# A deformable gather's row weights: one 128-partition transfer and a two-sided clamp in place of four 32-partition transfers, an upload through TensorE and two clamps

## The reference, cut to what matters

```
off = _conv(x, ow, 1) + ob
py = clip(yy + off[:, :, 0], 0.0, H - 1)      # row coordinate of every output pixel
px = clip(xx + off[:, :, 1], 0.0, W - 1)      # column coordinate
y0, x0 = floor(py), floor(px);  wy, wx = py - y0, px - x0
out = v00*(1-wy)*(1-wx) + v01*(1-wy)*wx + v10*wy*(1-wx) + v11*wy*wx
```

## Time and profile before

| | us |
|---|---|
| runs | 5919.41, 5877.91, 5885.14 |
| median | 5885.14 |
| span of the profiled execution | 5921.8 |
| first gather, from its first row DMA to its end | 1185.8 |
| second gather | 340.1 |
| third gather | 302.7 |
| middle stage between the first and the second gather | 133.0 |
| middle stage between the second and the third | 160.2 |

### The profile page before, as it was taken

One profiled execution on the slowest core, in us unless ns is written; L12 is line 12 of the kernel. 1 busy time (PEld: TensorE's weight loads), 2 busy tenths in 40 slices (PEclk: granted clock), 3 DMA queues, 4 the chain that ended last, 5 costly groups with the idle time before them and its releaser, 6 DMA issues. The chain is left out here.

```text
span 5921.8 us, 79668 instructions
## 1 busy us (share of the span) xinstructions
PE 5032.9 (85%) x30592; PEld 2727.3 (46%) x30592; DVE 3610.3 (61%) x4317; ACT 1856.8 (31%) x2899; POOL 1464.4 (25%) x1828
## 2 busy tenths in 40 slices
PE   4877877876999799997998995999999967986987
PEld 2333333324777677766776772222222233232222
DVE  6888878885666566653222223767677765653764
ACT  2222222202222122210000003667677743641750
POOL 0222222230000000002001002555555543442540
PEclk7888888867999899998999997889799887777987
DMA  1000000001000000002211216889899968857962
GB/s 30 15 15 22 22 22 22 15 15 72 15 15 8 22 1 14 15 19 100 68 61 65 75 50 153 205 196 211 181 219 216 210 171 174 185 121 137 215 172 92
DMA packets 272018, 538.25 MB, mean 91 GB/s; under 512 B 167976, under 2 KB 169576, under 8 KB 264728
## 3 DMA queue, kind: packets, MB, share of 16 engines
q1 hardware_dynamic: 271640, 533.13, 36.3%
HBM read 419.75 MB, written 113.25 MB: 90 GB/s over the span
## 5 line engine op out<-in xcount | busy, mean ns | idle before, releaser
L1436 POOL TENSOR_SCALAR g_kw<-g_kw 128x512 f32<-128x512 f32 x1536 | 947.0, 641 | 904.3 <-ACT g_kw L1422 666.3
L1422 ACT ACTIVATE g_vw<-ps,l_index 128x512 f32<-128x512 f32 x1536 | 970.0, 685 | 409.5 <-PE ps L1478 409.4
L1455 DVE SCALAR_TENSOR_TENSOR g_prod<-g_vw,ps 128x1024 f32<-128x1024 f32 x768 | 902.7, 1217 | 271.4 <-PE ps L1493 270.8
L1296 PE MATMUL ps<-o_pad,o_ow 128*128 128x512 f32 x3456 | 851.8, 408 | 8.4 <-DVE o_pad L822 7.7
L1478 PE MATMUL ps<-g_coord,l_spread 80*128 80x512 f32 x1920 | 743.2, 489 | 125.2 <-DMA g_coord<-coords 125.1
L1093 PE MATMUL ps<-l_pair,l_w 128*128 128x512 f32 x3072 | 779.8, 403 | 0.0
L1478 PEld LDWEIGHTS ps<-g_coord,l_spread 80*128 80x128 f32 x1920 | 343.2, 213 | 906.3 <-ACT g_vw L1422 679.6
L1296 PEld LDWEIGHTS ps<-o_pad,o_ow 128*128 128x128 f32 x3456 | 656.8, 191 | 197.9 <-DVE o_pad L822 7.9
L1093 PEld LDWEIGHTS ps<-l_pair,l_w 128*128 128x128 f32 x3072 | 575.7, 191 | 156.4 <-issue 29.4
L1422 ACT ACTIVATE g_kw<-ps,l_index 128x512 f32<-128x512 f32 x384 | 264.3, 688 | 1176.3 <-PE ps L1478 1162.1
L1493 PE MATMUL ps<-g_kw,g_img 32*32 32x512 f32 x12288 | 508.9, 687 | 126.2 <-DVE g_prod L1455 100.0
(11 more groups left out here) (247 smaller groups left out, 4737.7 us busy)
## 6 DMA issues: line engine op xcount, KB each, us to landing
g_rows<-whole SPq DMA_DIRECT2D x1536, 192.0 KB, 4.9
coords<-o_parts SPq DMA_DIRECT2D x32, 1024.0 KB, 4.0
g_coord<-coords SPq DMA_DIRECT2D x96, 256.0 KB
l_x<-xcur SPq DMA_DIRECT2D x16, 1024.0 KB, 6.1
coords<-o_parts SPq DMA_DIRECT2D x32, 512.0 KB, 5.6
g_img<-dense SPq DMA_DIRECT2D x96, 128.0 KB, 4.4
gathered<-g_res SPq DMA_DIRECT2D x48, 256.0 KB, 4.7
l_xn<-in_x SPq DMA_DIRECT2D x8, 1024.0 KB, 5.0
```

The lines of the kernel that those rows point to most:

```text
L1296: ins = nc.tensor.matmul(ps[:, lo:lo + HALF], ow[:, a, kk, tap, y, k * P:(k + 1) * P], padded_rows(pad[:, m, c, kk], j, tap), start=(n == ...
L1422: nc.scalar.activation(to, bank(a % RING), ACT.Relu, bias=index[:, 0:1]).then_inc(sem("ring_read"), 1)
L1436: nc.gpsimd.tensor_scalar(part, part, 1.0, 0.0, ALU.min, ALU.max).then_inc(sem("clamped"), 1)
L1455: nc.vector.scalar_tensor_tensor(prod[:, n % PB, 2 * half:2 * half + 2, :].rearrange("p r n -> p (r n)"), vw[:, n % VB, 2 * half:2 * half ...
```

## The change

Row coordinates no longer come in four pieces of 32 partitions. `whole` is stored once for every band of 8 rows, with 8 times the band's number subtracted, so that it holds 4 blocks x 4 bands = 16 copies of rows, and one DMA (L1362 of the changed kernel) takes 16 source rows of 8 KB, each repeated for 8 partitions, to all 128 partitions: 1 MB for a quad, all four channels. `rows` has 5 buffers and is clamped in place with two limits for each partition (`clamp`: row%8 - 1 and row%8, and 1 and 1 for row 0), one channel by GpSimd and three by DVE. The weight so made differs from the ramp by a constant of each row, and `ramp_base` puts the opposite into row 0 of the steps (a sum over rows and a sum over the bands' last rows, on DVE). The "k" task, `load_rows`, `kw` and the row half of `coords` are gone; the 16 partitions of `coord` that it used are set to zero once.

```diff
@@ Coordinates
+        if rows is not None:
+            for b in range(1, BANDS):
+                ins = ts(self.bands[rows, slot, b - 1, :], pos[rows], -float(b * BAND), None, ALU.add)
+        if columns is not None:
+            high, low = (self.parts2[columns, slot, j, :] for j in range(2))
+            link(nc.vector.tensor_copy(high, pos[columns]))
+            ins = nc.vector.tensor_tensor(low, pos[columns], high.bitcast(F32), ALU.subtract)
...
+def ramp_base(nc, link, out, tails, rows):
+
+    link(nc.vector.tensor_reduce(out, rows.rearrange("p y w -> p w y"), AX, ALU.add))
+    link(nc.vector.tensor_reduce(tails, rows[:, BAND - 1:SIDE:BAND, :].rearrange("p y w -> p w y"), AX, ALU.add))
+    link(nc.vector.scalar_tensor_tensor(out, tails, -float(BAND), out, ALU.mult, ALU.add))
+    return nc.vector.tensor_tensor(out, out, rows[:, SIDE - 1, :], ALU.add)
...
@@ build_gather
-        KB, VB, PB, SB = 3, 2, 2, 3
+        VB, PB, SB = 2, 2, 5
...
                 def send_rows(q):
                     s, j, g = quads[q]
                     if q >= SB:
-                        sp.wait_ge(sem("sent_relu"), q - SB + 1)
-                    t, h = divmod(g, 2)
-                    for r in (0, 2, 1, 3):
-                        lo = r * SIDE + 8 * t + channel_of(h, 1)
-                        sp.dma_start(rows[r * SIDE:(r + 1) * SIDE, q % SB].rearrange("p c n -> p (c n)"),
-                                     whole[s, j, lo:lo + 3].rearrange("q n -> (q n)").partition_broadcast(SIDE))\
-                          .then_inc(sem(f"rows_sent{q % SB}"), 16)
+                        sp.wait_ge(sem("rows_summed"), q - SB + 1)
+                    sp.dma_start(rows[:, q % SB].rearrange("p c n -> p (c n)"),
+                                 whole[s, j, :, :, 4 * g:4 * g + 4, :].rearrange("r b c n -> (r b) (c n)")
+                                 .unsqueeze(1).to_broadcast([UNITS * BANDS, BAND, 4 * HALF]))\
+                      .then_inc(sem(f"rows_sent{q % SB}"), 16)
...
-                def load_rows(s):
-                    for t in range(4):
-                        sp.dma_start(coord[CM:CROWS, s % 2, t].bitcast(F32),
-                                     coords[s, 0].rearrange("(r t q) s n -> t r q s n", r=4, t=4)[t, :, 0:2]
-                                     .rearrange("r q s n -> r (q s) n")).then_inc(sem(f"coord_loaded{s % 2}"), 16)
...
             def _(pool):
+                nc.gpsimd.memset(coord[CM:CROWS, :, :, :].bitcast(F32), 0.0).then_inc(sem("coord_zero"), 1)
+                pool.wait_ge(sem("coord_zero"), 1)
                 for q in range(Q):
-                    for c in range(4):
-                        if c == 0:
-                            pool.wait_ge(sem("ring_read"), at["k", q, 0] + 1)
-                        else:
-                            pool.wait_ge(sem("sent_relu"), q + 1)
-                        part = kw[:, q % KB, c, :]
-                        nc.gpsimd.tensor_scalar(part, part, 1.0, 0.0, ALU.min, ALU.max).then_inc(sem("clamped"), 1)
+                    pool.wait_ge(sem(f"rows_sent{q % SB}"), 16 * (q // SB + 1))
+                    part = rows[:, q % SB, 0, :]
+                    nc.gpsimd.tensor_scalar(part, part, clamp[:, 0:1], clamp[:, 1:2], ALU.max,
+                                            ALU.min).then_inc(sem("first_clamped"), 1)
...
-                def relu(q):
-                    dve.wait_ge(sem(f"rows_sent{q % SB}"), 64 * (q // SB + 1))
-                    if q >= KB:
-                        dve.wait_ge(sem("rows_summed"), q - KB + 1)
-                    nc.vector.tensor_scalar(kw[:, q % KB, 1:4, :].rearrange("p c n -> p (c n)"),
-                                            rows[:, q % SB].rearrange("p c n -> p (c n)"), index[:, 0:1], 0.0, ALU.add,
-                                            ALU.max).then_inc(sem("sent_relu"), 1)
+                def clamp_rows(q):
+                    dve.wait_ge(sem(f"rows_sent{q % SB}"), 16 * (q // SB + 1))
+                    part = rows[:, q % SB, 1:4, :].rearrange("p c n -> p (c n)")
+                    nc.vector.tensor_scalar(part, part, clamp[:, 0:1], clamp[:, 1:2], ALU.max,
+                                            ALU.min).then_inc(sem("rest_clamped"), 1)
...
@@ build_middle, SP
-                        for y in range(2):
-                            half = slice(m % 2 * CM, (m % 2 + 1) * CM)
-                            sp.dma_start(coords[bass.ds(turn * (PASS // 2) + m // 2, 1), y, half, :, :]
-                                         .rearrange("a p s n -> (a p) s n"),
-                                         co.stored(slice(y * CM, (y + 1) * CM), m)).then_inc(sem(f"coords_stored{m}"), 16)
-                        sp.dma_start(whole[bass.ds(turn * (PASS // 2) + m // 2, 1), :, half, :].rearrange("a j p n -> (a p) j n"),
-                                     co.pos[0:CM, m % 2, :].rearrange("p (j n) -> p j n", j=NH)).then_inc(sem(f"coords_stored{m}"), 16)
+                        half = slice(m % 2 * CM, (m % 2 + 1) * CM)
+                        sp.dma_start(coords[bass.ds(turn * (PASS // 2) + m // 2, 1), half, :, :]
+                                     .rearrange("a p s n -> (a p) s n"),
+                                     co.stored(slice(CM, P), m)).then_inc(sem(f"coords_stored{m}"), 16)
+                        for r in range(CM // SIDE):
+                            for b in range(BANDS):
+                                sp.dma_start(whole[bass.ds(turn * (PASS // 2) + m // 2, 1), :, m % 2 * (CM // SIDE) + r, b]
+                                             .rearrange("a j p n -> (a p) j n"),
+                                             co.band(slice(r * SIDE, (r + 1) * SIDE), m, b)).then_inc(sem(f"coords_stored{m}"), 16)
```

More of the change, by code:

```diff
@@ L33 @@
 CROWS = 80
+BANDS = 4
+BAND = SIDE // BANDS
 IMGS = 4
@@ L1380, in _ @@
                     load_columns(0, r)
-                load_rows(0)
                 load_image(0)
-                send_rows(1)
-                send_rows(2)
+                for q in range(1, SB):
+                    send_rows(q)
                 for q in range(SB, Q):
@@ L1941, in constants @@
         "row_of": (tok // SIDE).astype(np.float32), "col_of": (tok % SIDE).astype(np.float32),
-        "sel_spread": spread, "sel_fold": fold,
+        "sel_spread": spread, "sel_fold": fold, "row_clamp": clamp,
         "grid_token": tok.astype(np.float32),
```

182 lines of the change are left out of this document (93 added, 89 removed).

## The result

| | us |
|---|---|
| changed kernel, 4 runs | 6204.41, 6156.63, 6193.18, 6207.47; median 6198.8 |
| kernel before, beside it | 5919.41, 5877.91, 5885.14, 5949.27; median 5902.3 |
| ratio | 1.048, 95% interval 1.042 to 1.054: slower |
| span of the profiled execution (6204.41) | 6202.8, against 5921.8 before |

What follows compares the result with a forecast made beforehand. It took the gathers to be bound by a 3.81 us PSUM loop a quad plus stalls for rows. 5921.8 - 225 (gathers) + 4 (first offsets stage) + 50 (middle stages) = 5751 profiled, stated as 5720 us; range 5640 to 6090.

Steps and rivals of the forecast that it cites:

- the rate of the row transfer: Gathers: the 1 MB DMA at 388 GB/s costs 2.7 us a quad, with other transfers 3.2, under 3.81.
- The rival with chance 0.30: Gathers: row transfer stays at 231 to 252 GB/s, 4.7 us a quad; 5990, or 6145 at mean 5.1; chance 0.30.
- the cover of `ramp_base`: First offsets stage: 1.9 us each, beside convolutions except for each turn's first image, 4 us in all.
- `load_rows` gone: Gathers: without its four DMAs the want of rows at the end of each set goes; no separate size.
- the floor of 3.81 us: Gathers: the loop over four undoubled PSUM banks takes 3.81 us a quad, 1463 us for 384, untouched by the change.
- DVE's clamp: Gathers: two limits from memory instead of one make it 1.08 us, DVE's sum 3.43, under 3.81.
- the middle stages: Both middle stages: band copies, ramp_base and more stores add 50 us, bounds 25 to 110.
- the 4 us off the head of a gather: Start of each gather: without load_rows the 18.8 us before the first spread shrink by 4 us.
- a slow quad with four spreads: Gathers at 1.2 GHz: one spread fewer takes a quad from 6.55 to 5.95 us.
- the 225 us for the gathers: Three gathers: from 1828.6 to 1604 us, 225 gained, 100 to 265 by the bounds.
- the 40 us of stalls: Gathers: stalls that stay, one quad in twenty at 5.95 us, 40 us; bounds none and 165.
- GpSimd's clamp: Gathers: GpSimd loses three of four clamps of 641 ns and is not the bound at 3.81.

Runs made afterwards that it cites:

- near16: Changed kernel with the row transfer's 16 source rows 8 KB apart in DRAM instead of 64 KB, each still read 8 times: 6202 us.
- pad_distinct: Changed kernel with source rows padded to 36 channels, the row transfer reading 16 rows by 8 different rows, nothing read twice: 6205 us.
- one_row_128: Changed kernel with a row transfer that reads one row of 8 KB 128 times, to 128 partitions: 5822 us.
- outer32: Changed kernel with a row transfer of 32 source rows, 32 KB apart, each read 4 times; other data than the reference's: 5885 us.
- spread_loads: stored_twice with a set's img loads issued one a quad from the sixth quad, column loads at the tenth, twelfth, fourteenth and sixteenth: 5732.5 us, ratio 0.965.
- eight_of_16: Changed kernel with its row transfer cut into 8 transfers of 128 KB, each taking the 16 source rows once to every eighth partition: 6407 us.
- ramp_later: Changed kernel with the first offsets stage's ramp_base calls moved on DVE from inside the norm to behind the third kind's positions: 6135 us.
- stored_twice: Changed kernel with each row stored twice, so the transfer has 32 rows outermost, each read 4 times, and ramp_later's order: 5834.9 us, ratio 0.984.
- before_rows_once: Kernel before the change with load_rows called only for the first two sets, ahead of the loop: 5914 us, against 5942 beside it.
- pool_immediates: Changed kernel with constants 0 and 8 as the limits of GpSimd's clamp instead of two values from memory: 6207 us.

## Why the prediction was wrong

**The step that failed is the rate of the row transfer**: "So the new DMA costs 1.05/388 = 2.7 us for a quad ... I take 3.2: it is the same partition count as the row with 388, and I see the partition count and nothing else separate 388 from 231 and 252." Partition count was the same in all of near16, pad_distinct, one_row_128 and outer32; what separated 560 from 310 ns a packet was whether 16 or at least 32 rows stood outermost in the transfer's pattern. The row packets take 4.48 us a quad and all others 0.66, together 5.14, where the prediction had 2.7 and 0.5, together 3.2. The measured gathers are 2005.9/384 = 5.22 us a quad, heads included. The rival with chance 0.30 described it, priced to a mean of 5.1 in its bad case, 6145. That the measured time lies only 54 us above is partly luck: the stages around the gathers took 51 us more than the rival had for them and the gathers 27 less, and the profiled span lies 4 us above the median where 36.7 had been carried over.

The 3.2 was too low for the fast form as well: 3.30 and 0.62, together 3.92, in outer32, and 3.74 in spread_loads. Taking 388 GB/s for the average of a quad leaves out that the packets grow longer beside other transfers.

Why 16 differs is argued, not shown. The Trainium skill, "DMA: Bandwidth & Descriptors", section "Why a DMA increments its semaphore by 16 and not by 1", has a transfer use as many engines as divide the slowest dimension of both sides: 16 in each of these forms, so the count is not it. The same page of the Trainium skill, section "The descriptor swizzle", gives each engine a port of its own for 128 partitions. If 16 shares of a pattern with 16 rows are 8 neighbouring partitions each, then by the Trainium skill, "SBUF — State Buffer", section "Door 1: The DMA port swizzle", partitions 32 apart share a port, and the shares of partitions 0 to 7 and 32 to 39 meet. The factor of 1.8 in the packets' medians fits that. By that map the every eighth partition of eight_of_16 reaches 8 of 16 ports, and it moved 209 GB/s; but its DMA share was 0.87 there, as issuing held it back too, so it says little. No trace here shows which engine wrote which partition.

**The second step that failed is the cover of `ramp_base`**: "It lies beside convolutions except for the first image of each turn: 2 x 1.9 = 4 us." It lies beside convolutions, but ahead of positions that TensorE was about to need: before the change DVE had freed PSUM only just in time. Measured 58 us ahead of the first gather, and ramp_later, where only the place is another, starts it 52 us earlier. The other 6 are about the 7 by which the first image's positions stand later in it too; the start of that image differs by 10 us between kernels that do the same up to there (ramp_later 2731.4, stored_twice 2721.5), so they have no cause that the runs show. Its length was also 2.8 and not 1.9 us, the strided sum alone 1.86 to 2.04.

**`load_rows` gone**: "With them goes the want of rows at the end of each set." Half right at most. Without it the gathers took 38 us less and the whole kernel 28 less, in one run of before_rows_once, within the spread of the kernel before; the `img` and column loads made a stall of their own ahead of it, which rows 4 did not show because I opened the timeline at the last load and not at the first.

**Right:** the floor of 3.81 us (changed kernel and spread_loads both reach it where rows are there); DVE's clamp, 1.079 us against 1.08; the middle stages, 46 us against 50; with a fast form, the 4 us off the head of a gather (25.4 us before, 20.1 in outer32); a slow quad with four spreads, 6.1 us in stored_twice's timeline against 5.95, and 6.55 before. **Too good:** the 225 us for the gathers. With a fast form and the loads where the change has them they give up 1739 - 1611 = 128 us from first to last weigh step in outer32 and 173 in stored_twice, as more than the 40 us of stalls stay. Only with the loads spread is it 1739 - 1469 = 270. **Wrong without effect:** GpSimd's clamp is 2.87 us, where I had kept 0.64 for it, hidden behind weigh (done at 4406.61, weigh at 4407.02); the head of the first gather is 24.5 us in the changed kernel, not 4 us shorter. The forecast of 5720 for the change as it was made stays wrong. That spread_loads measures 5732 is the work of further edits (a form with 32 rows, `ramp_base` moved, the loads spread), less the cost of the second stores; that it comes so near 5720 is chance.

## What to carry to other kernels

Read the rate of a DMA off a transfer with the same access pattern, outermost count included, not off one with the same partitions; if the trace has none, measure that one transfer first, since here two forms of the same bytes to the same partitions differed by 1.8 in the median packet. Then add up what all transfers need in the stretch that matters, because packets grow longer beside others (309 ns in the median, 419 in the mean). For work added to an engine with idle time, look at what stands behind it in that engine's order and who waits for that: 5.8 us for an image on an engine that idled 21.5 us soon after cost 7 to 8, and nothing one kind later. And follow a stall back to its first long interval, not to the transfer that happens to be nearest to its end.

## What the runs showed of the hardware

- A 1 MB load to 128 partitions: 8 KB packets of 549 to 560 ns in the median with 16 rows outermost (near16, pad_distinct, changed), 309 to 312 ns with 32, 64 or 128; means 551 to 565 and 403 to 419 ns. Reading one 8 KB row 128 times was not slower than reading 128 rows.
- GpSimd's clamp of 128x512 took 612 ns in the median of the kernel before (constants 1 and 0, minimum first) and 1.92 us in pool_immediates (constants 0 and 8, maximum first), whether or not a clamp of DVE's overlapped it. With two limits from memory it took 2.07 us without such an overlap and 2.87 when started with DVE's clamp, DVE's staying at 1.08; in pool_immediates DVE's took 1.47. The Trainium skill, "GPSIMD Engine Reference", section "1. Specifications", has the two engines share SBUF interfaces; these rows agree that each can lengthen the other's work.
- DVE's sum over a strided tile, 128x1024 to 32, took 1.86 to 2.04 us, against 0.695 for a clamp with constants over as many elements (L1133, median before).
- Issuing a DMA from SyncE took 0.54 us for the 1 MB transfer (changed) and 0.59 in the median for each 128 KB piece of it (eight_of_16): pieces are not cheaper to issue.
